# Cross attention for 16 sequences: part of the normalisation moved to GpSimd, weights loaded in pieces, new instruction orders, filler matmuls at the end

## The reference

```
q = x @ Wq + bq; k = ctx @ Wk + bk; v = ctx @ Wv + bv
scores = einsum('bkgld,bksd->bkgls', q, k) / 4 + mask
out = softmax(scores) @ v                      # per head, then heads side by side
z = out @ Wo + bo + x
x1 = (z - mean(z)) * rsqrt(var(z) + 1e-6) * gamma + beta
# second layer, one head of width 512
q1, k1, v1 = x1 @ w_q.T, ctx @ w_k.T, ctx @ w_v.T
result = x1 + alpha * (softmax(q1 @ k1.T / sqrt(512)) @ v1) @ w_o.T
```

## Time and profile before

| | us |
|---|---|
| median of 3 runs | 739.95 (734.6 to 741.24) |
| profiled execution, whole | 737.84 |
| its span, first to last instruction | 736.1 |
| PE busy | 669.4 (91%) |
| DVE busy | 512.7 (70%) |
| ACT busy | 393.5 (53%) |
| POOL busy | 369.4 (50%) |

### The profile page before, as it was taken

The page is one execution under the profiler, slowest core; times in us unless marked ns, Lnnn a source line. Parts: engine busy times, 40 slices in busy tenths (PEclk is TensorE's granted clock), DMA queues, the critical chain, the costliest instruction groups (busy, mean ns, idle before and its releaser), DMA issues.

```text
span 736.1 us, 11738 instructions
## 1 busy us (share of the span) xinstructions
PE 669.4 (91%) x3658; PEld 462.2 (63%) x3658; DVE 512.7 (70%) x1467; ACT 393.5 (53%) x589; POOL 369.4 (50%) x225
## 2 busy tenths in 40 slices
PE   5998998989999999999989999999999989897756
PEld 2556656666676767776758677676767656563434
DVE  1258879778696869786857778696978778754120
ACT  2324766645566656666655656475666636564100
POOL 3454766545556564646455565556555534554000
PEclk9999999999999999999999999999999989999987
DMA  7696685755768685858493758678687644541500
GB/s 285 254 145 132 158 128 174 148 155 133 151 148 202 139 188 118 219 124 196 134 194 116 195 127 205 144 172 177 134 198 160 140 141 82 97 151 47 170 9 12
DMA packets 60856, 110.51 MB, mean 150 GB/s; under 512 B 11661, under 2 KB 50125, under 8 KB 60026
## 3 DMA queue, kind: packets, MB, share of 16 engines
q1 hardware_dynamic: 60794, 109.76, 63.2%
HBM read 86.79 MB, written 22.52 MB: 149 GB/s over the span
## 4 chain that ended last, share of the span: by engine, by line
PE 49%; DMA 23%; DVE 9%; issue 8%; SPq 7%; POOL 2%; ACT 1%; POOLq 0%; DVEq 0%; ACTq 0%
PE mx_ps L543 7%; PE work L505 6%; PE work L507 5%; PE work L506 5%; DMA qs<-mt_l 5%; PE work L626 5%; PE o_ps L559 5%; DMA late<-r_dr 4%; DMA r_dr<-rden 4%; DMA o_dr<-o_s 3%; PE work L616 3%; DMA k_dr<-k_l 3%; DVE mx_ps L1439 2%; DVE late L1482 2%; PE sc_ps L526 2%
## 5 line engine op out<-in xcount | busy, mean ns | idle before, releaser
L1439 DVE CUSTOM_DVE_ANT_0 mx_ps<-mx_ps,mask_n 100x361 f32<-100x361 f32 x512 | 270.2, 544 | 90.7 <-PE mx_ps L543 87.9
L2327 POOL TENSOR_TENSOR pr<-pr,mask_t 128x800 f32<-128x800 f32 x128 | 249.5, 1962 | 162.8 <-ACT pr L1912 162.6
L543 PE MATMUL mx_ps<-ks,qs 96*100 96x362 f32 x512 | 182.9, 379 | 12.9 <-DVE mx L1439 9.7
L1912 ACT ACTIVATE pr<-sc_ps 128x800 f32<-128x800 f32 x128 | 106.9, 835 | 106.1 <-PE sc_ps L531 59.7
L1918 ACT ACTIVATE pr<-pr 128x1200 f32<-128x1200 f32 x128 | 152.1, 1203 | 12.0 <-POOL pr L2327 7.2
L543 PEld LDWEIGHTS mx_ps<-ks,qs 96*100 96x100 f32 x512 | 85.2, 168 | 50.5 <-DVE mx L1439 25.8
L1425 DVE TENSOR_TENSOR pr<-sc_ps,mask_t 128x400 f32<-128x400 f32 x128 | 73.0, 571 | 17.5 <-PE sc_ps L526 10.6
L559 PE MATMUL o_ps<-pr,va 128*32 128x400 f32 (+1 forms) x768 | 72.7, 512 | 3.4 <-ACT pr L1918 3.4
L1439 DVE DVE_READ_ACCUMULATOR2_ANT mx<- 100x1 f32 x512 | 72.1, 141 | 0.0
L626 PE MATMUL work<-n_w,late 128*100 128x512 f32 x128 | 69.4, 635 | 1.5 <-ACT late L1984 1.4
L2339 POOL TENSOR_TENSOR c_l<-cT,c_h 128x1448 fp32r<-128x1448 f32 x16 | 53.6, 3350 | 29.7 <-ACT c_h L1939 29.7
(11 more groups left out here) (121 smaller groups left out, 1149.3 us busy)
## 6 DMA issues: line engine op xcount, KB each, us to landing
qs<-q_dr SPq DMA_DIRECT2D x128, 100.0 KB, 4.8
late<-in_ctx SPq DMA_DIRECT2D x16, 768.0 KB, 4.7
cT<-in_ctxT SPq DMA_DIRECT2D x16, 724.0 KB, 5.9
ks<-k_dr SPq DMA_DIRECT2D x128, 90.5 KB, 4.4
late<-in_ctxT SPq DMA_DIRECT2D x16, 724.0 KB, 5.2
o_dr<-o_s SPq DMA_DIRECT2D x32, 200.0 KB, 3.7
xT<-in_xT SPq DMA_DIRECT2D x16, 200.0 KB, 3.2
y<-in_x SPq DMA_DIRECT2D x16, 200.0 KB
```

The costliest lines, as they stand in the source:

```text
L543: nc.tensor.matmul(mx_ps[0:L, n % 2, 0:SP2], qs[p][0:TERMS, g, L * j:L * (j + 1)], ks[p][0:TERMS, g, 0:SP2], start=True, stop=True).then_i ...
L1439: V.tensor_tensor_reduce(out=src, in0=src, in1=mask_n[p][:, :], scale=1.0, scalar=-3.0e38, op0=ALU.add, op1=ALU.max, accum_out=mx[p][:, n: ...
L1912: A.activation(pr[:, g % 4, 1:3, :], sc_ps[:, 1:3, 0:JL], ACT.Copy).then_inc(sc_cp, 1)
L2327: G.tensor_tensor(t, t, mask_t[p][:, 1:3, :].unsqueeze(2).to_broadcast([P, 2, J, L]), ALU.add).then_inc(sc_pool, 1)
```

## The change

Five things, in the order of the diff.

- The weights of the first fold come in four pieces of 512 columns each, with a semaphore for each, and `fold_m` waits piece by piece; Wq, Wk and Wv have semaphores of their own. SP's first DMAs have a new order.
- `normalize` and `o_low` run on POOL instead of DVE.
- `centre`, `gain` and `shift` become two `scalar_tensor_tensor` operations: `centre` computes (y - mean) * gamma and needs no deviation, `shift` multiplies by the deviation and adds beta.
- The lists of calls of all five engines are in new orders.
- `keep_busy(count)` issues matmuls whose result is not read, into `mx_ps`, after the last maximum; 56 of them in 15 places of the last two batches.

```diff
+            def fold_m_in(o):
+                cs = slice(512 * o, 512 * (o + 1))
+                sp.dma_start(st[:, 512 * o:512 * (o + 1)], w1q_d[:, cs]).then_inc(w_1[o], 16)
+                sp.dma_start(st[:, 2048 + 512 * o:2048 + 512 * (o + 1)], w1k_d[:, cs]).then_inc(w_1[o], 16)
...
             for i in range(4, 13):
-                stacks_in(i, 1, 0, 2)
+                stacks_in(i, 1, 2, 4)
                 reciprocals_out(i - 2)
...
+            def keep_busy(count):
+                pe.wait_ge(a_mx, NH * B)
+                for _ in range(count):
+                    nc.tensor.matmul(mx_ps[0:L, 0, :], wq_h[:, 0, 0:L], wq_h[:, 0, :], start=True, stop=True)
...
             y_part(14, 0, 4)
+            keep_busy(3)
             values(15, 1)
             turn_x1(14)
+            keep_busy(5)
             xm_part(14, 0, 4)
+            keep_busy(2)
             turn_xm(14)
+            keep_busy(1)
             s1_part(14, 0, 4)
+            keep_busy(6)
             turn_p1(14)
+            keep_busy(2)
             cx_part(14, 0, 4)
+            keep_busy(1)
             d_part(14, 0, 4)
+            keep_busy(3)
             y_part(15, 0, 4)
+            keep_busy(16)
             turn_x1(15)
...
             def centre(b):
-                dve.wait_ge(rstd_ok, b + 1)
                 dve.wait_ge(mv_ok, b + 1)
-                V.tensor_scalar(y[:, :], y[:, :], mv[:, 0:1], rstd[:, 0:1], ALU.subtract, ALU.mult).then_inc(xc_ok, 1)
-
-            def gain(b):
+                if b == 0:
+                    dve.wait_ge(w_s, 64)
+                V.scalar_tensor_tensor(y[:, :], y[:, :], mv[:, 0:1], gamma_b[:, :], ALU.subtract, ALU.mult).then_inc(xc_ok, 1)
+
+            def shift(b):
...
+                dve.wait_ge(rstd_ok, b + 1)
...
+                V.scalar_tensor_tensor(x1[p][:, :], y[:, :], rstd[:, 0:1], beta_b[:, :], ALU.mult, ALU.add).then_inc(x1_ok, 1)
...
+            def normalize(b):
+                pool.wait_ge(ot_in, 16 * (b + 1))
+                pool.wait_ge(rb_in, 16 * (b + 1))
+                G.tensor_tensor(r_b, o_l[:, :].bitcast(F32), r_b, ALU.mult).then_inc(on_ok, 1)
+
+            def o_low(b):
+                pool.wait_ge(oh_ok, b + 1)
+                G.tensor_tensor(o_l[:, :], r_b, o_h[:, :].bitcast(F32), ALU.subtract).then_inc(ol_ok, 1)
```

More of the change, by code:

```diff
@@ L842, in _ @@
             scores(0, 7, 0, 1)
-            heads(1, 16, 18)
-            turn_maxima(1, 0)
             v_part(2, 0, 1)
-            heads(1, 18, 21)
+            heads(1, 18, 20)
             v_part(2, 1, 2)
-            heads(1, 21, 22)
+            heads(1, 20, 22)
             v_part(2, 2, 3)
-            heads(1, 22, 23)
+            heads(1, 22, 24)
             v_part(2, 3, 4)
+            scores(1, 0, 1, 3)
+            heads(1, 24, 26)
+            values(0, 1)
+            heads(1, 26, 27)
@@ L911, in _ @@
+            v_part(3, 0, 1)
+            scores(2, 0, 0, 3)
+            v_part(3, 1, 2)
             values(1, 1)
-            v_part(3, 0, 1)
-            heads(2, 24, 26)
-            v_part(3, 1, 2)
+            heads(2, 26, 28)
+            turn_x1(0)
+            v_part(3, 2, 3)
             scores(2, 1, 1, 3)
-            v_part(3, 2, 3)
-            turn_x1(0)
-            heads(2, 26, 27)
             v_part(3, 3, 4)
+            heads(2, 28, 30)
+            xm_part(0, 0, 1)
             scores(2, 2, 1, 3)
-            heads(2, 27, 29)
@@ L922, in _ @@
[L922 to L933 removed]
+            xm_part(0, 1, 2)
+            heads(2, 30, 31)
+            xm_part(0, 2, 3)
+            heads(2, 31, 32)
+            xm_part(0, 3, 4)
@@ L1087, in _ @@
                 heads(i, 27, 28)
+                xm_part(i - 2, 0, 1)
+                heads(i, 28, 29)
                 scores(i, 2, 1, 3)
-                heads(i, 28, 29)
-                scores(i, 1, 0, 1)
-                xm_part(i - 2, 0, 1)
                 heads(i, 29, 30)
@@ L1120, in _ @@
-                heads(i + 1, 9, 10)
-                scores(i, 4, 1, 3)
-                heads(i + 1, 10, 11)
-                q_part(i + 2, 2, 3)
-                cx_part(i - 2, 0, 1)
+                heads(i + 1, 6, 7)
+                scores(i, 4, 1, 3)
+                heads(i + 1, 7, 8)
+                q_part(i + 2, 2, 3)
+                heads(i + 1, 8, 9)
+                turn_p1(i - 2)
+                q_part(i + 2, 3, 4)
+                heads(i + 1, 9, 10)
+                values(i, 0)
@@ L1154, in _ @@
+            scores(12, 7, 1, 3)
+            heads(13, 18, 20)
             y_part(11, 0, 1)
@@ L1208, in _ @@
-            turn_p1(11)
             q_part(15, 2, 3)
             heads(14, 8, 10)
+            values(13, 0)
+            scores(13, 4, 0, 1)
+            turn_p1(11)
+            heads(14, 10, 11)
+            scores(13, 4, 1, 3)
             q_part(15, 3, 4)
             cx_part(11, 0, 1)
+            heads(14, 11, 13)
+            cx_part(11, 1, 2)
             scores(13, 5, 1, 3)
-            cx_part(11, 1, 2)
-            heads(14, 10, 12)
             cx_part(11, 2, 3)
+            heads(14, 13, 14)
@@ L1230, in _ @@
-            d_part(11, 3, 4)
-            k_part(15, 0, 1)
-            heads(14, 17, 18)
-            scores(13, 7, 1, 3)
-            k_part(15, 1, 2)
-            heads(14, 18, 19)
-            turn_maxima(14, 0)
-            k_part(15, 2, 3)
-            heads(14, 19, 20)
-            k_part(15, 3, 4)
+            heads(14, 17, 18)
+            k_part(15, 0, 1)
+            heads(14, 18, 19)
+            d_part(11, 3, 4)
+            k_part(15, 1, 2)
+            heads(14, 19, 21)
+            k_part(15, 2, 3)
@@ L1240, in _ @@
+            turn_maxima(14, 0)
+            k_part(15, 3, 4)
+            heads(14, 21, 22)
+            scores(13, 7, 0, 1)
             y_part(12, 0, 1)
-            heads(14, 20, 21)
+            heads(14, 22, 23)
             y_part(12, 1, 2)
-            heads(14, 21, 22)
+            heads(14, 23, 24)
             y_part(12, 2, 3)
-            heads(14, 22, 23)
+            heads(14, 24, 25)
             y_part(12, 3, 4)
+            scores(14, 0, 0, 1)
+            values(13, 1)
             scores(14, 0, 1, 3)
-            scores(14, 0, 0, 1)
@@ L1289, in _ @@
+            turn_p1(12)
+            values(14, 0)
             cx_part(12, 0, 1)
[L1290 removed]
+            heads(15, 9, 10)
             cx_part(12, 1, 2)
[L1292 to L1302 removed]
@@ L1303, in _ @@
-            heads(15, 15, 16)
-            d_part(12, 2, 3)
-            scores(14, 6, 0, 1)
-            d_part(12, 3, 4)
+            scores(14, 5, 0, 1)
+            cx_part(12, 2, 3)
+            heads(15, 10, 11)
+            cx_part(12, 3, 4)
+            scores(14, 6, 0, 1)
+            scores(14, 5, 1, 3)
+            heads(15, 11, 13)
+            d_part(12, 0, 1)
+            heads(15, 13, 14)
+            d_part(12, 1, 2)
+            heads(15, 14, 15)
+            d_part(12, 2, 3)
+            heads(15, 15, 16)
@@ L1328, in _ @@
-            scores(15, 1, 0, 1)
-            xm_part(13, 0, 1)
-            scores(15, 2, 0, 1)
             xm_part(13, 1, 2)
```

1373 lines of the change are left out of this document (665 added, 708 removed).

## The result

The changed kernel takes 701.46 us in the median of 4 runs (698.44 to 702.24), beside 740.6 us of the kernel before on the same chip: a ratio of 0.9476, 95% interval 0.9412 to 0.9539. On a second chip it was 698.59 us, 0.948 (0.94 to 0.956). 27 us less had been forecast (713), some 39 came.

A forecast was written before the change was run, and what follows sets the result against it. PE bounds the loop, running 1.5 us a batch above its 37.9 us floor. Terms 8 + 10 + 1.2 + 6.5 + 1.5 + 4 = 31 us, less 5 charged, give 26 off 737.84: 712, stated as 713 against the median; range 701 to 729.

The forecast's parts named there:

- The maxima's DMA: Loop: turned maxima no longer queue behind the output rows and context on SP; 8 of 10.9 us of waits, bounds 0 and 10.9.
- rival B: The maxima's wait moves from half 1 to half 0, so 8 us become about -3: 724 us, chance 0.15.
- Normalisation to POOL: Multiplication leaves DVE, where POOL's work had stretched it, so PE waits less for maxima: 10 us, bounds 6 and 14.
- The blocked stretch: Around 585 to 592 us, a 5.96 us multiplication on DVE held the maxima: 8 us with the clock loss.
- rival D: POOL becomes late because reciprocals arrive late, delaying masks and what follows: 747 us, chance 0.05.
- The layer norm's end: Fewer DVE operations behind the deviation: 0.6 us in each of two serial batches, 1.2 in all, nothing in the loop.
- The end: Last 38 us: fillers in PE's idle stretches keep the clock full, 6.5 us, bounds 0 and 7.5.
- 650 to 698 us: Earlier exponential 2, clock 1.5, reciprocals 3.5 us earlier, less a 2 us hold of `d_part(14)` behind `o_high(15)`: 1.5 us net.
- The start: First fold starts near 3.8 us instead of 8.15, `heads(0, 0)` near 44 instead of 48.5: 4 us, bounds 0 and 7.
- The charge for new waits: Deduction for unseen waits that the five new orders might create: 5 us, bounds 0 and 12.
- C: Orders do all they could, loop at PE's floor (13 us), no new wait: 35 us gained, 703 us, chance 0.13.
- E: The gains are eaten by new waits of the same size: 735 us, chance 0.10.

The follow-up runs named there:

- the first profile: Changed kernel, nothing altered, profiled on the first chip: that execution took 702.21 us.
- the experiment, which delays more than the pieces: Changed kernel with the first fold's four pieces loaded ahead of all other loads and awaited together: 703.87 us, 0.960 of the kernel before.
- the second profile: Changed kernel, nothing altered, profiled on a second chip, where its time was 698.59 us.

## Why the prediction held, and where it did not

The sign, the places and most mechanisms were right; the gain was under-sized by some 12 us, and the experiments show that its sum was of a form that cannot be relied on. That the time still fell into the range is in part luck: one of the largest gains, in batches 0 to 3, had no term, and on the second chip the median (698.59) is outside.

**The maxima's DMA (8 us).** The wait went wholly, 10.9 us, and rival B (it moves to half 0) did not come: PE never waits for `qs<-mt_l` in the first profile, and once, 0.6 us, in the second. The context was rightly named as a cause. But as a price of the part by itself, 8 us is refuted both ways: undone it cost 5.7%, done alone it cost 4.7%. The forecast also priced the wait alone: a third or more of what both runs lost in the loop is longer busy time of PE at a lower granted clock.

**Normalisation to POOL (10 us).** Right in sign; its size depends on the orders: 7 us alone (3 to 11), 19 undone (13 to 25), and 10 lies between. Its parts add up to 10.6. The split was partly wrong. The blocked stretch gave 5.2 of the 8 us; the half of the loop's waits that I gave to it (2.5) is 5.0 us on the old orders (347.8 instead of 352.8) and nothing in the new ones, whose loop hardly changes; and it works in batches 2 and 3, where I had given it nothing. No DVE multiplication of two SBUF operands is beside POOL's masks any more, but one DVE operation of 1.46 us a batch is left (below), so "over 2 us" held in the loop. POOL's multiplication ends 5.3 us ahead of `turn_maxima` (342.05 against 347.37), in the forecast 3.9: rival D shows nowhere in the changed kernel.

**The layer norm's end (1.2 us).** Right in the serial batch 15 (0.63; in batch 14 `values(15, 1)` is later and hides it), and wrong at "nothing in the loop". In the trace of before `x1` is ready 0.44 us ahead of `turn_x1`, 9.7 us behind `turn_maxima(i, 0)`. In the changed kernel it is ready at the same 9.7 us, and PE comes to `turn_x1` 0.4 us before that: one part each of the k and v projections and one head less stand ahead of it. The forecast did not ask how close the new order puts it.

**The end (6.5 us).** 7.0 us behind `turn_x1(15)`, fillers alone, shown on both orders.

**650 to 698 us (1.5 us).** 5.2 us in the traces from `turn_maxima(15, 0)` to `y_part(15)` (2.8 and 2.4), of which the forecast had 3.5 before its subtraction. The hold of 2 us did not exist. `o_high(15)` ran from 664.29 to 664.83 and `cx_part(14)` ended at 665.05: the low part's source was ready 2 us earlier against `cx_part(14)` than I had counted.

**The start (4 us).** 3.8 in the two profiles, some 3 over all of them; the experiment, which delays more than the pieces, cost 5. PE first worked at 5.08 us instead of the forecast 3.8.

**Batches 0 to 3 (no term).** 8.1 us, some 10 over all profiles, the largest single error. The trace of before shows it, in this row of the windows view:

```profile
115.71:162.37 46.66, 41.48 (x233) 29.51 (x231) 37.63 (x97) 26.35 (x39) 24.65 (x14) 0.96 0.70 179
```

Between `turn_maxima(2, 0)` and `(3, 0)` PE was idle 5.2 us at a clock of 0.96; now that stretch takes 38.5 us. I had cut the profile into start, loop and end, and this stretch was in none. In the kernel before, POOL alone took 2.8 us off batches 2 and 3, and its return to DVE in the changed kernel cost 6.4 there; how the rest divides among the orders was not tried.

**The charge for new waits (5 us).** The waits in the loop are now `turn_x1`'s 3.3 us and 2.2 us for the next batch's stacks (in the second profile 3.1 and 0.3). With the removed waits it left PE 5.5 us idle in the loop, 4.0 in the second profile, of 11.6. The loop's gain of 5.8 us in the first profile equals the forecast's 5.5, but in four others it is 8 to 10: mostly the charge was not needed.

Of the rivals, C came out nearest (703), though not by its account: the loop gave 6 to 10 us and not 13, the rest came from batches that no case had. E, "eaten by new waits of the same size", is what happens when the parts are put on the old orders.

## What to carry to other kernels

A part of a joint schedule need not have a price of its own: here the maxima's place in SP's list, undoing which costs 5.7% in the finished kernel, cost 4.7% when the lists around it stayed, and the normalisation's engine was worth 7 us in one set of lists and 19 in the other. Before moving a waiting DMA forward in a single issuing queue, find what it will hold while it waits (here 6.9 us of sums, residual and stacks) and move that ahead of it first. Price every stretch of the span, also the ones between "start" and "loop", and for each consumer that the new order moves, ask how close to its producer it now stands. When a wait of PE is priced, look at the granted clock too: in three of these runs a third to a half of the loss was PE's longer busy time at a lower clock. Two parts could be added by themselves, at 1% each: the fillers, which took back the same 7 us behind `turn_x1(15)` in both sets of lists, and the normalisation on POOL.
